# Attention sums divided straight from PSUM, split into two fp16 parts and transposed by DMA; projection as fp16 products

## What is computed

```python
def _L0_xattn_ref(x, context, Wq, Wk, Wv, Wo, bo):
    q = (x @ Wq).reshape(B, Nq, HEADS, DIM_HEAD).transpose(0, 2, 1, 3)
    k = (context @ Wk).reshape(B, Nc, HEADS, DIM_HEAD).transpose(0, 2, 1, 3)
    v = (context @ Wv).reshape(B, Nc, HEADS, DIM_HEAD).transpose(0, 2, 1, 3)
    sim = jnp.einsum('bhid,bhjd->bhij', q, k) * SCALE
    attn = jax.nn.softmax(sim, axis=-1)
    out = jnp.einsum('bhij,bhjd->bhid', attn, v)
    out = out.transpose(0, 2, 1, 3).reshape(B, Nq, HEADS * DIM_HEAD)
    return out @ Wo + bo
x = x + _L0_xattn_ref(_layernorm(x, axis=-1), ctx_768, Wq, Wk, Wv, Wo, bo)
```

## Time and profile before

| | |
|---|---|
| median of 3 runs | 2167.38 us |
| lowest, highest run | 2164.70 us, 2167.46 us |
| profiled execution, first to last instruction | 2169.9 us |
| PE busy | 2103.3 us (97%) |
| POOL busy | 1933.6 us (89%) |
| ACT busy | 1832.2 us (84%) |
| DVE busy | 1736.7 us (80%) |

### The profile page before, as it was taken

How to read it: one execution, slowest core, us unless ns; L and a number is a source line. 1 busy time by engine, 2 the same in 40 slices (tenths; PEclk the granted TensorE clock), 3 DMA queues, 4 the chain that set the end, 5 groups by cost and what they waited for, 6 DMA issues and landing times.

```text
span 2169.9 us, 58374 instructions
## 1 busy us (share of the span) xinstructions
PE 2103.3 (97%) x22087; PEld 1544.3 (71%) x22087; DVE 1736.7 (80%) x4158; ACT 1832.2 (84%) x3124; POOL 1933.6 (89%) x1127
## 2 busy tenths in 40 slices
PE   8999999999999999999999999999999999999998
PEld 4677777777777777777777777777777777777665
DVE  7778878787887888879687797878878788886764
ACT  6898898989888888998888888898878888888872
POOL 3899999999999899999899998998989999899991
PEclk9999999999999999999999999999999999999999
DMA  3110000000000000000000000000000000000000
GB/s 73 42 38 13 2 13 2 2 13 2 13 2 2 13 2 13 2 13 2 11 13 2 13 2 2 14 2 13 2 11 13 2 13 2 2 2 2 2 11 11
DMA packets 17366, 22.10 MB, mean 10 GB/s; under 512 B 5872, under 2 KB 14976, under 8 KB 17088
## 3 DMA queue, kind: packets, MB, share of 16 engines
q1 hardware_dynamic: 15984, 18.17, 3.0%
q10 hardware_dynamic: 1104, 0.20, 0.1%
HBM read 16.14 MB, written 2.10 MB: 8 GB/s over the span
## 4 chain that ended last, share of the span: by engine, by line
PE 76%; DVE 11%; issue 5%; ACT 5%; POOL 2%; DMA 0%; SPq 0%; DVEq 0%; ACTq 0%; POOLq 0%
PE PS L573 14%; PE PS L613 13%; PE PS L574 13%; PE PS L590 11%; PE PS L592 10%; PE PS L636 4%; DVE EH L1091 4%; PE PS L646 2%; PE PS L623 2%; DVE over L1114 2%; POOL EL L1566 2%; ACT PF L897 2%; PE PS L657 1%; ACT over L919 1%; DVE junk L1359 1%
## 5 line engine op out<-in xcount | busy, mean ns | idle before, releaser
L1566 POOL TENSOR_TENSOR EL<-PF,EH 124x1024 f16<-124x1024 f32 x828 | 1761.7, 2153 | 144.0 <-DVE EH L1091 69.4
L897 ACT ACTIVATE PF<-PS 124x512 f32<-124x512 f32 x1664 | 972.6, 602 | 203.7 <-PE PS L574 190.1
L590 PE MATMUL PS<-Ch,EH 123*128 123x97 f16 (+1 forms) x6656 | 765.8, 207 | 22.9 <-POOL EL L1566 22.2
L592 PE MATMUL PS<-Cl,EL 123*128 123x97 f16 (+1 forms) x6656 | 762.3, 207 | 0.0
L1091 DVE TENSOR_SCALAR_CACHE_REDUCE EH<-PF 124x1024 f16<-124x1024 f32 x621 | 746.1, 1209 | 18.1 <-ACT PF L897 16.9
L590 PEld LDWEIGHTS PS<-Ch,EH 123*128 123x128 f16 (+1 forms) x6656 | 609.1, 98 | 181.5 <-issue 62.7
L1114 DVE CUSTOM_DVE_ANT_1 over<-over,PS 128x806 f32<-128x806 f32 x512 | 506.6, 989 | 284.7 <-ACT over L919 142.8
L592 PEld LDWEIGHTS PS<-Cl,EL 123*128 123x128 f16 (+1 forms) x6656 | 597.8, 98 | 168.2 <-issue 1.9
L573 PE MATMUL PS<-AH,ChT 97*124 97x512 f16 x1664 | 646.6, 389 | 6.5 <-ACT PF L897 5.8
L574 PE MATMUL PS<-AL,ClT 96*124 96x512 f16 x1664 | 633.7, 381 | 0.0
L919 ACT ACTIVATE over<-PS 128x806 f32<-128x806 f32 x512 | 433.4, 846 | 28.6 <-PE PS L613 8.6
(11 more groups left out here) (248 smaller groups left out, 1766.9 us busy)
## 6 DMA issues: line engine op xcount, KB each, us to landing
Cf<-in_ctx SPq DMA_DIRECT2D x16, 546.0 KB
X<-in_x SPq DMA_DIRECT2D x16, 128.0 KB, 2.4
out_x<-X SPq DMA_DIRECT2D x16, 128.0 KB, 1.7
msk<-in_attention_mask SPq DMA_DIRECT2D x4, 256.0 KB, 4.3
AH<-mh SPq DMA_DIRECT2D x63, 2.0 KB
Cf<-in_ctx SPq DMA_DIRECT2D x16, 53.6 KB
xWqT<-in_xWqT SPq DMA_DIRECT2D x2, 256.0 KB, 6.5
xWo<-in_xWo SPq DMA_DIRECT2D x2, 256.0 KB, 4.3
```

The costliest lines, as they stand in the source:

```text
L590: pe.matmul(PS[:, 6, u0:u0 + DC + 1], EH[0:kr, r, qs], Ch[j][0:kr, t, :], start=(t == 0 and q == 0), stop=False, skip_group_check=True)
L592: m = pe.matmul(PS[:, 6, u0:u0 + DC + 1], EL[0:kr, r, qs], Cl[j][0:kr, t, :], start=False, stop=(t == KT - 1), skip_group_check=True)
L897: act.activation(PF[:, n % PRING, :], PS[0:KP, 4 + n % 2, :], ACT.Exp).then_inc(sg("ex"), 1)
L1566: pool.tensor_tensor(EL[:, r - 1:r + 1, :], PF[:, f - 1:f + 1, :], EH[:, r - 1:r + 1, :], ALU.subtract).then_inc(sg("lo_pool"), 1)
```

## The change

1. ACT's copy of the sums (U), and POOL's multiplication, are gone. DVE takes the reciprocals straight from bank 6 and multiplies from bank 6 into Un (`norm`), in its list beside the pair's last `av`, three tiles earlier than its reciprocal stood. PE's next pair waits for `un`, raised by this multiplication.
2. A new step `u_split`, two tiles later (SPLIT_LATER): ACT rounds Un to the high fp16 part, POOL subtracts to get the low one, both into UHL (fp16, 128 x 1536 for a quad).
3. `turn_u` leaves PE. SP issues one DMA transposition of UHL to UT (twelve 128 x 128 blocks), in its list four tiles after the quad's last `av` (TURN_LATER). It waits for both `ul` (POOL's part) and the last projection. SP gets a list of its own, with the stores six tiles later.
4. `proj` stands eight tiles after the quad's last `av` (PROJ_LATER) and is twelve fp16 products of 128 x 128, of the high parts by MH and the low parts by ML. The scale goes to DVE's addition to X.
5. Once, in the first batch, M is scaled and split to MH and ML (`m_max`, `mtop`, `msplit`).
6. In `sel_rank` (16 times) a fused two-input operation on DVE becomes two small scalar ones, and `keep` gets an accumulator output.
7. 24 filling products stand before the last projection in place of five.

```diff
-            "ctx_lo": 1, "ln0": 1, "ln_stats0": -3, "ln_stats1": -2, "ln_stats2": -1, "norm": 1, "q": 1,
+            "ctx_lo": 1, "ln0": 1, "ln_stats0": -3, "ln_stats1": -2, "ln_stats2": -1, "q": 1,
...
-            "ln_stats2": 3, "norm": 3},
+            "ln_stats2": 3},
+    "sp": {"c_scat": 6},
...
-        if done >= 2 and (done - 2) % KT == 0:
-            put(n, "norm", (done - 2) // KT)
-        for late, step in ((-2, ("turn_u", 0)), (2, ("turn_u", 1)), (5, ("proj",))):
-            late += KT
-            if done >= late and (done - late) % (2 * KT) == KT:
+        if done >= 0 and done % KT == 0 and done // KT < B * HP - 1:
+            put(n, "norm", done // KT)
+        if done >= 0 and done % KT == SPLIT_LATER:
+            put(n, "u_split", done // KT)
+        for later, kind in ((TURN_LATER, "turn_u"), (PROJ_LATER, "proj")):
+            if done >= 0 and done % (2 * KT) == KT + later:
...
                     if t == 0 and n > 0:
-                        w.wait_ge(sg("u"), b * HP + hp)
+                        w.wait_ge(sg("un"), b * HP + hp)
...
                         for c in range(QC):
-                            m = pe.matmul(PS[:, kb, t * D:(t + 1) * D], UT[:, t, c, :], M[:, qd * QC + c, :],
-                                          start=(c == 0), stop=(c == QC - 1))
+                            for part, of in enumerate((MH, ML)):
+                                m = pe.matmul(PS[:, kb, t * D:(t + 1) * D], UT[:, (part * T + t) * QC + c, :],
+                                              of[:, qd * QC + c, :], start=(c == 0 and part == 0),
+                                              stop=(c == QC - 1 and part == 1))
...
-                elif k == "turn_u":
-                    b, qd, t = s.a
-                    w.wait_ge(sg("un"), min(b * HP + 2 * qd + 2, LAST_SUMS))
...
-                    for c in range(QC):
-                        m = pe.transpose(PS[:, kb, c * P:(c + 1) * P],
-                                         Un[qd % 2][:, t, :, :].rearrange("p h c -> p (h c)")[:, c * P:(c + 1) * P],
-                                         ident[:, :])
...
-                        act.activation(U[x % 2][:, :, :], PS[:, 6, 0:4 * (DC + 1)].rearrange(
-                            "p (q c) -> p q c", c=DC + 1), ACT.Copy).then_inc(sg("u"), 1)
...
+                elif k == "u_split":
+                    x, = s.a
+                    b, qd = x // HP, x % HP // 2
+                    w.wait_ge(sg("un"), x + 1)
+                    w.wait_ge(sg("ut"), 16 * max(0, b * QD + qd - 1))
+                    act.activation(UHL[qd % 2][:, 0, :, 2 * (x % 2):2 * (x % 2) + 2, :], Un[x % 2][:, :, :, :],
+                                   ACT.Copy, scale=KEEP).then_inc(sg("uh"), 1)
...
+                    w.wait_ge(sg("av"), (x + 1) * KT)
+                    dve.reciprocal(rden_u[:, x % 2, :], sums[:, :, DC]).then_inc(sg("u_r"), 1)
+                    w.wait_ge(sg("u_r"), x + 1)
+                    if x >= 2:
+                        w.wait_ge(sg("ul"), x - 1)
                     dve.tensor_tensor(
-                        Un[1][:, :, 2:4, :].rearrange("p t h c -> p h t c"),
+                        Un[x % 2][:, :, :, :].rearrange("p t h c -> p h t c"),
...
+                elif k == "turn_u":
+                    b, qd = s.a
+                    w.wait_ge(sg("ul"), b * HP + 2 * qd + 2)
+                    w.wait_ge(sg("pj_mm"), b * QD + qd)
+                    sp.dma_start(UT[:, :, :], UHL[qd % 2][:, :, :, :, :].rearrange("p w t h c -> p (w t h c)"),
+                                 transpose=True).then_inc(sg("ut"), 16)
```

More of the change, by code:

```diff
@@ L216, in put @@
         stream.append((n + shift.get(kind, 0), len(stream), (kind, *a)))
-    out += opening(engine)
+    out += opening("pe" if engine == "sp" else engine)
     groups, todo = beside_plan(), []
@@ L239, in whole_order @@
         done = n - AV_LAG - (KT - 1)
-        if done >= 2 and (done - 2) % KT == 0:
-            put(n, "norm", (done - 2) // KT)
-        for late, step in ((-2, ("turn_u", 0)), (2, ("turn_u", 1)), (5, ("proj",))):
-            late += KT
-            if done >= late and (done - late) % (2 * KT) == KT:
-                quad = (done - late) // (2 * KT)
-                put(n, step[0], quad // QD, quad % QD, *step[1:])
+        if done >= 0 and done % KT == 0 and done // KT < B * HP - 1:
[4 more added lines that the diff above has]
+            if done >= 0 and done % (2 * KT) == KT + later:
+                quad = done // (2 * KT)
+                put(n, kind, quad // QD, quad % QD)
     out += [step for _, _, step in sorted(stream)]
-    out += [("norm", B * HP - 1), ("turn_u", B - 1, QD - 1, 0), ("turn_u", B - 1, QD - 1, 1), ("proj", B - 1, QD - 1)]
+    out += [("norm", B * HP - 1), ("u_split", B * HP - 1), ("turn_u", B - 1, QD - 1), ("proj", B - 1, QD - 1)]
     out += [("ln_stats2", B - 1), ("sel_w", B - 1), ("sel_row", B - 1)]
@@ L374, in build @@
         M = sb("M", [P, MC, D])
+        MH = sb("MH", [P, MC, D], F16)
+        ML = sb("ML", [P, MC, D], F16)
+        mmx = sb("mmx", [P, 1])
+        mtop = sb("mtop", [P, 1])
+        mscale = sb("mscale", [P, 1])
+        mback = sb("mback", [P, 1])
+        pback = sb("pback", [P, 2])
         rden_u = sb("rden_u", [P, 2, 4])
@@ L395, in build @@
         qscale = sb("qscale", [P, 2, 4, 2])
-        U = [sb(f"U{i}", [P, 4, DC + 1]) for i in range(2)]
-        Un = [sb(f"Un{i}", [P, T, 4, DC]) for i in range(2)]
-        UT = sb("UT", [P, T, QC, P])
+        Un = [sb(f"Un{i}", [P, T, 2, DC]) for i in range(2)]
+        UHL = [sb(f"UHL{i}", [P, 2, T, 4, DC], F16) for i in range(2)]
+        UT = sb("UT", [P, 2 * T * QC, P], F16)
         pmax = sb("pmax", [P, 2, H * T])
@@ L552, in tensor_program @@
                 k, i = s.kind, s.i
-                if (k, *s.a) == ("turn_u", B - 1, QD - 1, 0):
+                if (k, *s.a) == ("proj", B - 1, QD - 1):
                     w.wait_ge(sg("ex"), TOTAL)
@@ L669, in tensor_program @@
                                  ident[0:KP, 0:KP]).then_inc(sg("sg_mm"), 1)
+                elif k == "mtop":
+                    w.wait_ge(sg("mmx"), 1)
+                    kb = bank_free(s)
+                    pe.transpose(PS[:, kb, 0:P], mmx[:, :].to_broadcast([P, P]), ident[:, :]).then_inc(sg("mt_mm"), 1)
                 elif k == "gtop":
@@ L1125, in vector_program @@
                                              op0=ALU.mult, op1=ALU.subtract).then_inc(sg("q_lo"), 1)
-                elif k == "norm" and s.a[0] == LAST_SUMS:
+                elif k == "norm":
                     x, = s.a
                     sums = PS[:, 6, 0:4 * (DC + 1)].rearrange("p (q c) -> p q c", c=DC + 1)
-                    w.wait_ge(sg("av"), TOTAL)
-                    w.wait_ge(sg("un"), x - 1)
-                    dve.reciprocal(rden_u[:, x % 2, :], sums[:, :, DC]).then_inc(*own_step())
-                    w.wait_ge(*own_steps())
-                    w.wait_ge(sg("ut_mm"), T * (B * QD - 2))
+                    w.wait_ge(sg("av"), (x + 1) * KT)
[3 more added lines that the diff above has]
+                        w.wait_ge(sg("ul"), x - 1)
@@ L1151, in vector_program @@
                 elif k == "proj":
                     b, qd = s.a
+                    back = pback[:, b % 2:b % 2 + 1]
+                    if qd == 0:
+                        w.wait_ge(sg("m_back"), 1)
+                        w.wait_ge(sg("sigma"), b + 1)
+                        if b >= 2:
+                            w.wait_ge(sg("pj_x"), at["proj", b - 2, QD - 1])
+                        dve.tensor_scalar(back, u_scale[:, b % 4:b % 4 + 1], mback[:, 0:1], None, ALU.mult, ALU.add,
+                                          accum_out=spill()).then_inc(sg("pj_back"), 1)
@@ L1647, in sync_program @@
             sp.dma_start(rbc[:, :], row("router_b")).then_inc(sg("in_rows"), 16)
-            for s in order:
+            for s in orders["sp"]:
                 k, i = s.kind, s.i
```

114 lines of the change are left out of this document (53 added, 61 removed).

## The result

The change makes the kernel slower: 2390.64 us (median of 4 runs, 2385.87 to 2391.58) against 2166.59 us for the kernel before on the same chip, a ratio of 1.102 with a 95% interval of 1.101 to 1.104. The prediction was 2152 us, so it is wrong in sign and by 239 us, and outside its range. Further down, a time without a ratio stands on one run; over all runs beside them the kernel before read 2164.4 to 2174.0 us, so a few us between two single runs say nothing.

What follows compares the result with a forecast made beforehand. PE was taken as the bound, busy 97%, with POOL close behind. 2169.9 - 94 + 102 - 22 - 8 + 4 + 3 = 2155, less 2.5 us of profiling: 2152 us, range 2105 to 2236 (forecast case 2130 to 2180).

Steps and rivals of the forecast that it cites:

- PE is relieved: At PE's projections and half turns 135 us leave and 768 fp16 products cost 41 us: 94 us gained.
- The new wait at the pair ends: PE's next pair waits for two DVE operations instead of ACT's copy: 6.4 us lost per batch, 102 us in 16.
- What the waits cover: PE held at pair ends gives POOL time: -22 us of waiting for POOL, and -8 for bank 7 and ACT.
- POOL, ACT and DVE otherwise: POOL's subtraction replaces a multiplication of the same size, at no cost; ACT shorter; DVE 81 us longer against some 430 idle.
- The transposition: The DMA transposition takes 5.3 us, just inside the 5.4 us window before PE's projection, so it costs nothing.
- Both rivals on it: DMA transposition a little late (7.1 us): 2236 us, chance 0.09; very late (14.2 us): about 2700 us, chance 0.06.
- DVE is free sooner: Pair 2 loses only 1.0 us instead of 3.1, so 34 us less go: 2120 us, chance 0.25.
- The two terms for the ends: Last quad has no tiles to hide behind, +4 us; splitting M before the first batch's first projection, +3 us.
- DVE falls behind everywhere: EH stands behind each `norm` in DVE's list, POOL needs EH and PE needs POOL, +35: 2190 us, chance 0.18.

Runs made afterwards that it cites:

- part 1 alone: Kernel before, with DVE dividing the sums straight from PSUM and PE's next pair waiting for it; PE's transposes and fp32 projection stay: 2268.05 us.
- the split later: Changed kernel with the projection at 18 tiles, POOL's subtraction three tiles later and the transposition issued at 8 tiles: 2265.17 us.
- the normalisation first: Changed kernel with DVE's reciprocal and multiplication half a tile earlier, ahead of the EH and `fold` of their tile: 2318.57 us.
- all three places mended: Changed kernel with the projection at 18 tiles, subtraction and transposition later, and DVE's reciprocal and multiplication ahead of EH and `fold`: 2188.03 us.

## Why the prediction was wrong

**PE is relieved: right.** Predicted 135 - 41 = 94. Read from start to start as in the earlier trace rows, the 64 projections took 90.1 us before (1.405 to 1.442 us each), the turns 45.8 us, and the new projections take 43.3 us, so 92.6. The ledger has 85 for the same products, because it cuts each at its line's 20th percentile (85.2 + 41.8 = 127 us before, 42 after), and other products of PE, transposes mostly, take some 9 us more; that gives the 75 in the table.

**The new wait at the pair ends: the term was right, its places partly not.** Growth of the gap from a pair's last sum to the next pair's first, us per batch, in the mean of batches 1 to 15:

| pair | 2 | 4 | 5 | 6 | 8 | others | sum |
|---|---|---|---|---|---|---|---|
| predicted | 3.1 | 1.3 | in others | 1.0 | 0.6 | 0.4 | 6.4 |
| part 1 alone | 3.0 | 1.1 | 0.7 | 1.5 | 0.5 | 0.0 | 6.8 |
| after | 3.8 | 1.0 | 1.0 | 1.6 | 0.5 | 0.0 | 8.0 |

Reading in the trace when DVE would be free, `fold` first and `norm` behind it, gave 102 us where part 1 alone has 106 and the kernel after 123. Pair 5, which I had counted among those with nothing in front, has a burst of other DVE work there. The multiplication took 0.56 us where I took 0.63.

**"What the waits cover": right for part 1, wrong for the change.** The 22 us of waiting for POOL did vanish in the run with part 1 alone, but in the changed kernel they became 53. The projection's place has the larger part in that: moving it back brings them to 26.1 us, and the split later, which takes away POOL's wait for ACT's half, to 11.1. POOL's wait for ACT by itself doesn't settle it: with the normalisation first it fell from 136.9 to 45.5 us and PE's wait for EL stayed at 56.9.

**The half clock: a term that was not in the sum, +61 us.** I priced a wait at its length. In the kernel after, a long wait of PE comes with a stretch at 1.2 GHz, during it and behind it; part 1 alone shows +28 us of it beside +68 us of waits. I had the clock in the page in front of me and took it as given, as it was nearly full before (14.5 us of the span at half).

**The projection's place: the step that failed, about 100 us.** The sum has for all waits 102 - 22 - 8 + 4 + 3 = 79 us, the ledger 233. In front of the projection it has 67 us where the sum has none; in front of the sums' products 146 where the sum has 102 - 22. Under "what the waits cover" I wrote that bank 7 loses 128 users and counted relief, between 0 and 15 us. I never asked where the projection that stays would stand in the new order, only whether its transposition would have landed by then. The diff moves it by ten tiles, and the order of PE's list shows it one tile behind a `q` on the same bank. The run that moves it back gives 106 us, of them 27 that are also counted under the half clock and 27 of PE's waiting for EL, so these parts can't be added; the run that moves 48 of them in the old kernel gives 105.

**"POOL, ACT and DVE otherwise ... I cost it at nothing": sizes right, places not.** The subtraction is as long as the multiplication was (0.91 us), but it waits for ACT, whose half stands behind `over`, behind PE. Moving it later is worth 20 us.

**The transposition: right.** It lands in 3.7 us (predicted 5.3, window 5.4), and at most 7.6 us were waited for it in all. Both rivals on it, given 0.15 together, are refuted. So is "DVE is free sooner" (0.25): at pair 2 PE lost 3.8 us and not 1.0. The two terms for the ends (+4, +3) were not measured apart.

**The rivals.** "DVE falls behind everywhere" (2190 us, 0.18) lies nearest, and with all three places mended the kernel takes 2188 us; that the two numbers meet is luck. Its path was EH late, so EL late, so PE late, and PE's wait for EL is then 22.8 us, as before the change. What is left is waits straight for DVE and ACT in other places, which every further move handed on. Of the rival only the general idea, that DVE's lists have no slack, is borne out, and I had argued it down with DVE's 430 us of idle time. An idle share of 20% says nothing about slack within half a tile of a pair's end. The largest error of method was another: the sum was read at the places that the old list had, for a diff whose numbers 2, 4, 8 set new places.

## What to carry to other kernels

When a change writes new places for steps, look for each moved step at what shares its buffer or bank, one or two steps ahead in the new list: a short step right behind another user of the same bank costs PE a whole round trip through two engines (here about 1 us, and as much again in what comes late after it). Price a wait of PE that is longer than the trace has so far shown at more than its length, as the clock can fall with it. And a wait that moves from one line to the next at each attempt, at the same sum, is a sign to stop moving.

## What the runs showed of the hardware

- **A DMA that transposes 384 KB inside the chip** (128 x 1536 in fp16) lands in 3.7 us, where the loads of 256 KB for the mask land in 4.2 us in the same trace, and holds SyncE for 1.45 us. The Trainium skill's 1309 ns for one 128 x 128 block (VectorE: DVE Perf Modes, section "The three transpose paths") is therefore not a rate: twelve blocks take 0.31 us each here. Its 261 GB/s for a transposition with gaps in its pattern (DMA: Bandwidth & Descriptors, section "Latency and other measured facts") would be an estimate of 1.5 us for the data and leave 2.2 us besides; no run here varies the size, so that split is not shown.
- **Some DVE operations on SBUF wait for POOL.** The same multiplication takes 557 ns from PSUM and 1228 ns in the mean from SBUF. From SBUF 38 of the 128 took 560 ns or less too, and each of the other 90 ended 0.41 to 0.43 us after an instruction of POOL had ended. The operation `keep` on 2 elements took 2042 ns: 15 of its 16 ended less than 0.03 us after one of POOL's. The Trainium skill (SBUF — State Buffer, section "SBUF: two separate sides") says that VectorE and GpSimd share a pair of ports under an exclusive lock, held for a whole instruction; the trace agrees, and adds that freeing one instruction of it only passes the wait to the next such one (2042 ns to 150 ns, and 348 ns to 1178 ns behind it). So PSUM is the cheaper place for DVE to take the sums from, beside a POOL that is busy, even where it is the worse one for PE.
- **PE's granted clock fell within a wait** of 3.7 us, from the 2.4 to the 1.2 GHz level, and came back after 4.8 us of work at half speed. In all 15 standstills of over 3 us in the kernel after it fell before they ended. Shorter ones do not spare it: 14 of the other 16 stretches at half clock come with waits of 1.8 to 2.9 us. In the kernel before the longest wait of PE after its start is 1.72 us, and the clock stayed at 2.4 GHz but for 14.5 us.
